# Feed-forward of a Mamba and experts block: input chain half a group sooner, experts' rows gathered one group further ahead

## What is computed

```python
x = L0_attn_x                                   # 4 x 1024 x 256
x = layernorm(x + attn(x, ...))                 # Mamba-2 mixer, then 8 experts, top 2 of them per token
gate = silu((x @ w_gate) * s_gate)              # w_gate, w_up: 256 x 1024 int8
up = (x @ w_up) * s_up
x = layernorm(x + ((gate * up) @ w_down) * s_down)   # w_down: 1024 x 256 int8
```

## Time and profile before

| what | us |
|---|---|
| median of 3 runs (lowest, highest) | 1287.54 (1282.08, 1289.09) |
| profiled execution: its time | 1287.96 |
| profiled execution: its span | 1286.4 |
| TensorE matmul busy in the span | 1135.1 (88%) |
| VectorE, ScalarE, POOL busy | 687.0, 620.7, 369.0 |
| mean granted clock of TensorE | 0.953 |

### The profile page before, as it was taken

How to read it: one execution, slowest core, us unless ns; L and a number is a source line. 1 busy time by engine, 2 the same in 40 slices (tenths; PEclk the granted TensorE clock), 3 DMA queues, 4 the chain that set the end, 5 groups by cost and what they waited for, 6 DMA issues and landing times. The chain is left out here.

```text
span 1286.4 us, 21831 instructions
## 1 busy us (share of the span) xinstructions
PE 1135.1 (88%) x7496; PEld 1001.3 (78%) x7497; DVE 687.0 (53%) x1645; ACT 620.7 (48%) x1279; POOL 369.0 (29%) x328
## 2 busy tenths in 40 slices
PE   0799999899989998899999999999999268888896
PEld 0576768686767686799999999999999247777785
DVE  3576667676767665765322332332332256777654
ACT  1664656555555543354554454454454144444453
POOL 1203133333434243464321304044000432333300
PEclk9899999999999989889999999999999678889898
DMA  2020101010202011263313133121211321121101
GB/s 104 5 70 1 38 1 66 5 67 5 70 1 70 12 43 66 82 219 134 106 41 114 41 108 112 41 106 57 98 41 48 121 72 49 49 83 49 50 18 49
DMA packets 40386, 80.88 MB, mean 63 GB/s; under 512 B 6656, under 2 KB 30080, under 8 KB 39040
## 3 DMA queue, kind: packets, MB, share of 16 engines
q1 hardware_dynamic: 22816, 34.69, 8.2%
q0 software_dynamic: 7440, 35.66, 8.1%
q10 hardware_dynamic: 10064, 9.70, 2.2%
HBM read 48.31 MB, written 30.67 MB: 61 GB/s over the span
## 5 line engine op out<-in xcount | busy, mean ns | idle before, releaser
L1320 DVE TENSOR_TENSOR e_h_lo<-e_bank,e_h_hi 128x512 fp32r<-128x512 f32 x148 | 102.1, 691 | 287.8 <-ACT e_bank L641 285.3
L973 PE MATMUL e_bank<-e_x_hi,e_w_hi 128*128 128x256 f32 x592 | 169.7, 287 | 1.5 <-issue 1.3
L990 PE MATMUL e_bank<-e_w_hi,e_h_hi 128*128 128x256 f32 x592 | 170.6, 288 | 0.0
L974 PE MATMUL e_bank<-e_x_lo,e_w_hi 128*128 128x256 f32 x592 | 168.5, 285 | 0.0
L975 PE MATMUL e_bank<-e_x_hi,e_w_lo 128*128 128x256 f32 x592 | 168.4, 285 | 0.0
L992 PE MATMUL e_bank<-e_w_hi,e_h_lo 128*128 128x256 f32 x592 | 167.6, 283 | 0.0
L991 PE MATMUL e_bank<-e_w_lo,e_h_hi 128*128 128x256 f32 x592 | 167.5, 283 | 0.0
L1639 PE MATMUL f_bank<-f_x_hi,ffn_w 128*128 128x512 f32 x256 | 113.0, 441 | 31.4 <-DVE f_x_lo L1735 28.7
L639 ACT ACTIVATE e_h_hi<-e_bank 128x512 fp32r<-128x512 f32 x148 | 88.5, 598 | 78.4 <-PE e_bank L975 74.6
L1184 DVE SCALAR_TENSOR_TENSOR conv<-raw,conv_w,conv 128x512 f32<-128x512 f32 x120 | 96.0, 801 | 41.6 <-ACT conv L559 38.6
L973 PEld LDWEIGHTS e_bank<-e_x_hi,e_w_hi 128*128 128x128 f32 x592 | 114.5, 193 | 3.1 <-issue 3.1
(11 more groups left out here) (238 smaller groups left out, 2752.6 us busy)
## 6 DMA issues: line engine op xcount, KB each, us to landing
e_stage<-in_w POOLq DMA_DIRECT2D x9, 2048.0 KB
e_x_rows<-sent_rows SPq DMA_DIRECT2D x38, 256.0 KB
back_rows<-e_y_rows ACTq DMA_DIRECT2D x37, 256.0 KB, 2.1
x_in<-in_x SPq DMA_DIRECT2D x8, 512.0 KB, 4.0
x_res_dram<-x_res SPq DMA_DIRECT2D x8, 512.0 KB, 2.9
f_res<-x_res_dram SPq DMA_DIRECT2D x8, 512.0 KB, 3.4
out<-f_out_t SPq DMA_DIRECT2D x8, 512.0 KB, 2.8
back_rows<-zeros SPq DMA_DIRECT2D x8, 256.0 KB, 3.2
```

Source lines behind the costliest of these rows:

```text
L973: mm(out, w1h[:, k, t], x_hi[:, k], start=k == 0, stop=False)
L974: mm(out, w1h[:, k, t], x_lo[:, k], start=False, stop=False)
L990: mm(out, eh_hi[:, k, t], w2h[:, k], start=k == 0, stop=False)
L1320: tt(flat(eh_lo[:, 2 * p:2 * p + 2]), h_ps[p][:], flat(eh_hi[:, 2 * p:2 * p + 2]).bitcast(F32), ALU.subtract).then_inc(es["h_lo_ready"], 1)
```

## The change

The tile `mixed` gets a second buffer, and `mix_first(g)` waits for the normalizing of group g-2 instead of g-1. ScalarE normalizes the next group behind unit 1 instead of 3 and makes its high parts behind unit 4 instead of 6; TensorE transposes behind unit 2 instead of 4. In VectorE's `between` the mix for group g+2 moves to slots 1 and 2, its stats to slot 3, its moments to slot 7 and the shift to slot 0 of the next group; `x_parts` to slot 4. In group 0 the mix and the stats stand four slots later. POOL does `deviation(1)` and `gather(2)` ahead of its loop, and in the loop `gather(g + 3)` stands ahead of the `deviation` of group g+2.

```diff
--- before.py
+++ after.py
@@ -1481,7 +1481,7 @@
         s_down = sb("s_down", [P, D])
         back = sb("back", [P, 2, CH, 2, D])
         res = sb("res", [P, 2, CH, D])
-        mixed = sb("mixed", [P, CH, D])
+        mixed = sb("mixed", [P, 2, CH, D])
         bn = sb("bn", [P, 2, CH, 6])
         mv = sb("mv", [P, CH, 2])
         norm = sb("norm", [P, 3, CH])
@@ -1550,13 +1550,15 @@
             gather(0)
             gather(1)
             deviation(0, norm, "var_ready", "x1_ready", "rs_ready")
+            deviation(1, norm, "var_ready", "x1_ready", "rs_ready")
+            gather(2)
             for g in range(NG + 2):
-                if g + 1 < NG:
-                    deviation(g + 1, norm, "var_ready", "x1_ready", "rs_ready")
                 if g >= 2:
                     deviation(g - 2, norm2, "var2_ready", "out_ready", "rs2_ready")
+                if g + 3 < NG:
+                    gather(g + 3)
                 if g + 2 < NG:
-                    gather(g + 2)
+                    deviation(g + 2, norm, "var_ready", "x1_ready", "rs_ready")
 
         @block.scalar
         def _(act):
@@ -1573,7 +1575,7 @@
                 act.wait_ge(s["shift_ready"], g + 1)
                 if g >= X1_BUFS:
                     act.wait_ge(s["y_ready"], g - X1_BUFS + 1)
-                normalize(x1[:, g % X1_BUFS], mixed, norm, "x1_ready")
+                normalize(x1[:, g % X1_BUFS], mixed[:, g % 2], norm, "x1_ready")
 
             def scale2(g):
                 act.wait_ge(s["shift2_ready"], g + 1)
@@ -1602,9 +1604,9 @@
                     .then_inc(s["gate_ready"], 1)
                 if n:
                     part(n - 1)
-                if f == 3 and g + 1 < NG:
+                if f == 1 and g + 1 < NG:
                     scale1(g + 1)
-                if f == 6 and g + 1 < NG:
+                if f == 4 and g + 1 < NG:
                     x_parts(g + 1)
                 if f == 3 and g >= 2:
                     scale2(g - 2)
@@ -1661,7 +1663,7 @@
                     if g and 1 <= f <= KF // 2:
                         down(g - 1, 2 * f - 2)
                         down(g - 1, 2 * f - 1)
-                    if f == 4 and g + 1 < NG:
+                    if f == 2 and g + 1 < NG:
                         transposes(g + 1)
             for f in range(KF):
                 down(NG - 1, f)
@@ -1674,18 +1676,18 @@
             def mix_first(g):
                 dve.wait_ge(s[f"back_in{g % 2}"], 16 * 2 * CH * (g // 2 + 1))
                 dve.wait_ge(s[f"res_in{g % 2}"], 16 * (g // 2 + 1))
-                if g:
-                    dve.wait_ge(s["x1_ready"], g)
+                if g >= 2:
+                    dve.wait_ge(s["x1_ready"], g - 1)
                 for c in range(CH):
-                    i = stt(mixed[:, c], back[:, g % 2, c, 0], share[:, 0, CH * g + c:CH * g + c + 1],
+                    i = stt(mixed[:, g % 2, c], back[:, g % 2, c, 0], share[:, 0, CH * g + c:CH * g + c + 1],
                             res[:, g % 2, c], ALU.mult, ALU.add)
                 i.then_inc(s["mixed_one"], 1)
 
             def mix_second(g):
                 dve.wait_ge(s["mixed_one"], g + 1)
                 for c in range(CH):
-                    i = stt(mixed[:, c], back[:, g % 2, c, 1], share[:, 1, CH * g + c:CH * g + c + 1],
-                            mixed[:, c], ALU.mult, ALU.add)
+                    i = stt(mixed[:, g % 2, c], back[:, g % 2, c, 1], share[:, 1, CH * g + c:CH * g + c + 1],
+                            mixed[:, g % 2, c], ALU.mult, ALU.add)
                 i.then_inc(s["mixed_both"], 1)
 
             def stats(g, n, x, ready, done):
@@ -1753,41 +1755,42 @@
             def between(g, f):
 
                 if f == 0:
-                    if g >= 2:
-                        y_moments(g - 2)
-                    if g + 1 < NG:
-                        mix_moments(g + 1)
-                if f == 2:
                     if g + 1 < NG:
                         mix_shift(g + 1)
                     if g >= 2:
-                        y_shift(g - 2)
+                        y_moments(g - 2)
+                late = 4 if g == 0 else 0
+                if f == 1 + late and g + 2 < NG:
+                    mix_first(g + 2)
+                if f == 2 and g >= 2:
+                    y_shift(g - 2)
+                if f == 2 + late and g + 2 < NG:
+                    mix_second(g + 2)
                 if f == 3 and 1 <= g <= NG:
                     scale_down(g - 1, 0)
-                if f == 4 and g + 2 < NG:
-                    mix_first(g + 2)
-                if f == 5:
-                    if 1 <= g <= NG:
-                        scale_down(g - 1, 1)
-                    if g + 2 < NG:
-                        mix_second(g + 2)
+                if f == 3 + late and g + 2 < NG:
+                    stats(g + 2, 0, mixed[:, g % 2], "mixed_both", "mix_stats")
+                if f == 4 and g + 1 < NG:
+                    x_parts(g + 1)
+                if f == 5 and 1 <= g <= NG:
+                    scale_down(g - 1, 1)
                 if f == 6 and 1 <= g <= NG:
                     add_x1(g - 1)
-                if f == 7 and 1 <= g <= NG:
-                    stats(g - 1, 1, y[:, (g - 1) % 2], "y_ready", "y_stats")
-                if f == 6 and g + 1 < NG:
-                    x_parts(g + 1)
-                if f == 7 and g + 2 < NG:
-                    stats(g + 2, 0, mixed, "mixed_both", "mix_stats")
+                if f == 7:
+                    if g + 2 < NG:
+                        mix_moments(g + 2)
+                    if 1 <= g <= NG:
+                        stats(g - 1, 1, y[:, (g - 1) % 2], "y_ready", "y_stats")
 
             mix_first(0)
             mix_second(0)
-            stats(0, 0, mixed, "mixed_both", "mix_stats")
+            stats(0, 0, mixed[:, 0], "mixed_both", "mix_stats")
             mix_moments(0)
             mix_shift(0)
             mix_first(1)
             mix_second(1)
-            stats(1, 0, mixed, "mixed_both", "mix_stats")
+            stats(1, 0, mixed[:, 1], "mixed_both", "mix_stats")
+            mix_moments(1)
             x_parts(0)
             for n in range(NG * KF):
                 fuse(n)
```

## The result

| | before | after |
|---|---|---|
| median of 4 runs (lowest, highest) | 1284.88 (1282.08, 1289.09) | 1239.09 (1236.63, 1245.51) |
| profiled execution: time, span | 1287.96, 1286.4 | 1236.63, 1235.0 |
| first gather to the end of the span | 277.34 | 233.11 |

After takes 0.9649 of the time of before (95%: 0.9599 to 0.9698), 45.8 us less by the medians; a second measurement of the same two kernels, in the second series of experiments, gave 0.9668 (0.9634 to 0.9703), 1240.09 against 1284.21. The forecast was 1246, 41.7 us less than the 1287.54 of the first three runs. Of the 51.4 us between the two spans, 7.2 lie ahead of the feed-forward: in code that is the same, the first gather began at 1009.06 and at 1001.89 us. The change owns the **44.2 us** behind it, and all that follows is measured from there, as "the stage".

What follows compares the result with a forecast made beforehand. TensorE was taken as the bound, with x_lo waits at group starts and slow clock behind them. Gains of 1.1, 7.0, 2.8, 29.1 and 1.7 sum to 41.7 us, giving 1246; own range 1240 to 1252, widened to 1239 to 1256.

Steps and rivals of the forecast that it cites:

- head: Before the first unit: second mix needs only its rows, so x_lo is ready at 1036.4 instead of 1037.6, 1.1 us sooner.
- group 0: First group: from 24.98 us to 18.0, summed from units, transposes, their wait and a slow first unit; gain 7.0 us.
- group 1: Second group: from 29.91 us to 27.1, being 23.4 plus 2.0 of waits and 1.7 of slow clock; gain 2.8 us.
- groups 2 to 6: Middle groups: 23.4 us each without x_lo waits or slow clock, from 146.07 us to 117.0; gain 29.1 us.
- group 7 to the end: Last group: starts without idle and loses its slow stretch, priced like the tail's; gain 1.7 us, tail untouched.
- The walk through the queues: VectorE's queue in a middle group, slot by slot: x_lo ready at 18.4 us, needed at 23.4, 5 us to spare.
- its tightest place: Down product's first block: residue of unit 7 done at 28.3 us, wanted at 28.8, 0.5 us of slack.
- 8 times 0.2 for the slow first unit: Group 0's first unit: slow clock on its eight matmuls, a term in the group's 18.0 us.
- The wait that moves to the down block: First rival, down product's first block in every group: 1.2 us idle and 1.7 slow clock, 14.5 us, 1261; chance 0.1.
- The third, the port: Rival: each of a group's eight mixing instructions held 0.95 us for a gather, VectorE becomes the bound, 1272; chance 0.03.
- The second rival's place: POOL's pow held by gathers, VectorE's shift in slot 0 late before every fuse; slower, 1298 us; chance 0.02.
- the fourth, no effect: Rival: x_lo at group starts still late through some overlooked wait, 1286 us; chance 0.03.

Runs made afterwards that it cites:

- 0.6 us of load: Kernel after plus one VectorE multiplication of 512 columns that nobody reads in slot 7 of groups 0 to 7: stage 238.44 us.
- one buffer: Kernel after with one buffer of mixed rows and mix_first waiting for the group before: stage 250.50 us (disturbed), repeated 235.88 us, 0.9698 of before.
- the gathers alone: Kernel before with only POOL's new order, gathering group g+3 in turn g: 0.9939 of before, stage 273.05 us.
- 13 us of load: Kernel after plus twelve POOL pows that nobody reads ahead of the gathers of each of groups 3 to 7: stage 252.38 us.
- the parts back: Kernel after with scale1 behind unit 3, transposes behind unit 4 and both x_parts at unit 6 again: stage 247.87 us, group 0 disturbed.
- the mix put back: Kernel after with VectorE's mix for group g+2 back in slots 4 and 5, its stats in slot 7: stage 261.25 us, with stray waits.

## Why the prediction was right

Its sign, its mechanism and its size hold: x_lo's waits and the slow clock behind them are gone, and the gain is 45.8 us by the medians where 41.7 were forecast. That the absolute time is inside the range of 1239 to 1256 is luck in part: 1239.09 lies 0.1 us from its lower end and outside the forecast's own 1240 to 1252. Of the 6.9 us between it and 1246, 2.7 are the base, since with the fourth run the median of before is 1284.88 instead of 1287.54; 2.5 are terms of the sum, and the rest is what the medians gained beyond the stage. Term by term, in the stage:

| term | predicted gain | measured |
|---|---|---|
| head | 1.1 | 1.2 |
| group 0 | 7.0 | 6.2 |
| group 1 | 2.8 | 4.4 |
| groups 2 to 6 | 29.1 | 29.2 |
| group 7 to the end | 1.7 | 3.2 |
| sum | 41.7 | 44.2 |

**Groups 2 to 6** carry the forecast: 23.4 us a group was worked out from one side by counting matmuls and from the other by taking wait and slow clock from group 1 before, and 23.37 came. The walk through the queues held to 0.4 us at every point shown above, and its tightest place is real: 0.5 us of slack worked out, 0.26 in the rows of after, and 0.6 us of load turned it into a wait.

One reading of the prediction does not hold: that the 6.22 us at 0.50 in group 1 came behind the wait of 3.06 us. The clock had fallen before that wait, at 1059.85, behind the wait of 2.75 us that ended at 1059.24, and stayed low through both, 10.24 us in all. The second matmul from there is already as long as those at the lower level:

```profile
1060.20 0.63 PE L1640 MATMUL f_bank<-f_x_lo,ffn_w 128*128 128x512 f32 x1
```

As a price per wait, 3.1 us was the dearest case; in groups 2 to 6 it was 1.7 to 3.0. The sum did not suffer, since it took the middle groups' time from their starts.

**Group 1** was mis-sized. The step that failed is "TensorE waits in group 1 for a fuse (0.8) and for the last residue (1.2): 2.0 us, and ... 3.4 us of slow clock behind it". The waits are

```profile
1052.91 0.50 PE L1641 MATMUL f_bank<-f_x_hi,ffn_w 128*128 128x512 f32 x1 [0.57 <-DVE f_fused L1746]
1056.73 0.38 PE L1654 MATMUL f_bank<-ffn_w,f_f_hi 128*128 128x256 f32 x1 [0.96 <-DVE f_f_lo L1752]
```

1.5 us, and the clock stayed at 1.00. That it might was in the range, at 1.7 us. (The group is 2.1 us longer than a middle one, more than its waits, which are counted from modelled ends.)

**Group 0** came out 0.8 us short. The step was "8 times 0.2 for the slow first unit", 1.6 us. In the profiled execution the clock stayed at 0.50 beyond the first unit, for 4.9 us from the group's start, which cost 2.4:

```profile
1034.98 0.61 PE L1641 MATMUL f_bank<-f_x_hi,ffn_w 128*128 128x512 f32 x1
1035.40 0.42 PE L1642 MATMUL f_bank<-f_x_lo,ffn_w 128*128 128x512 f32 x1
```

(At the lower level such a row is 0.63 us long, at the upper 0.40.) That is the 0.8 us. When the clock rises differs between executions: with one buffer it did so 3.3 us into the group, and the group took 18.07.

**The tail** gave 1.5 us more than group 7's own slow stretch. Before and after have nearly the same two waits there, 0.57 and 1.41 against 0.55 and 1.39 us; before, 3.4 us at 0.51 followed, after it is 1.00 (the last stretch above). "The tail behind the last unit is untouched" was true of the code and not of the clock. These 1.5 us are luck and no gain of the change: behind such a wait of 1.4 us in the tail the clock fell in 3 of the 10 profiles that have one, in before, in one buffer's two, and in none of the others, the gathers alone among them.

The 1.6 us from these 44.2 to the 45.8 of the medians are inside the spread of the executions: the first gather starts anywhere from 1001.6 to 1019.6 us in the profiles of this study, in code that is the same in all.

**The rivals.** The wait that moves to the down block did not come, but it was the right first rival: 0.6 us more on VectorE calls it up. What the prediction held against it, that no such wait showed before, proved little. Before, the residue was ready 5.1 us into a group too, but TensorE came to it only 7.0 to 8.3 us in, being slowed by the clock; the change takes this time away with the slow clock. The third, the port, did not come either. Beside gathers, four mixes took 1.70 and 1.66 us, against 1.67 without them; of the four gathers issued meanwhile, two took 1.17 and 1.33 instead of 0.95. Over the whole profile, 47 single mixing instructions beside a gather have a median of 475 ns and at most 518, the 17 apart from gathers 477; the gathers' mean rose from 0.96 to 1.02 us. The Trainium skill (SBUF — State Buffer, the section SBUF: two separate sides) has a VectorE instruction with two inputs in SBUF and a GpSimd instruction that reads SBUF exclude each other, the later one blocked for the whole of the other. These rows do not agree for VectorE, and show for single gathers 0.2 to 0.5 us; whether issuing a gather counts as such an instruction, no run here shows. POOL had 8.67 us to spare. The second rival's place was reached only with 13 us of load, and the fourth, no effect, did not come.

**What each part is worth.** Alone, the gathers bring 4.3 us of stage. Taken out of the whole, they cost 41.4, the early mix some 26 to 28, the early parts 1.1 a group and the second buffer 1.8. These don't add up, as they are steps of one chain: rows, then mix, then x_lo. The mix early and nothing else, in the kernel before, was not tried.

## What to carry to other kernels

Walk the in-order queue of the engine that feeds the bottleneck, slot by slot, with the durations and the overlap of the trace: it gave every middle group to 0.1 us and named the place where a further 0.6 us of work costs 0.5 a group. A step can only be moved forward if its data come forward too; here the gathers alone brought 4.3 us of 44, and all the rest without them 2.5. Count the slow clock behind a wait as a second cost that may vanish with it. When it does, the bottleneck comes to its other operands earlier too (here 1.6 to 2.9 us to the last residue), so what never waited before may wait then. Measure from the stage's own start, since the same code ahead of it varies by more than single edits do.

## What was not expected of the hardware

**Where the clock falls.** The granted clock behind each wait of TensorE in the stage, over all profiles: behind single waits of at most 1.31 us it stayed at 1.00 each time (0.77 us in each of six groups of one run and 1.30 in each of five of another among them). Waits close together are another matter: with the parts back, waits of 1.42 and 1.01 us stood 1.2 us apart in the disturbed group 0, and the clock fell 0.35 us behind the second. Behind 1.4 to 2.3 us it went either way: with nearly the same wait of 2.22 to 2.26 us in the run of the mix put back, 3.4 us at the lower level followed in two groups and none in three. From 2.49 us on, the lower level followed or went on every time. Up to 6.2 us of it stood behind the wait of a group's start, and between two waits close together it did not end, as in group 0 of before. Prices from single cases: waits of 1.30 us made their groups 1.6 longer, those of 3.48 and 3.72 us ahead of groups 2 and 4 of before cost 5.2 and 6.7 with the slow clock, and 1.4 us in the tail cost 1.4 or 3.1. Why the middle sizes differ is open.

**Stray waits.** Three of the four profiles of the first series had waits of ScalarE and VectorE whose releaser the trace calls remote, up to 7.6 us each, in two of them in the experts' part too; before, after and the seven runs of the two later series had none. The first profile of one buffer was 15 us longer in the stage than the second, of the same code. They are not spread at random: in one buffer and in the mix put back they stand at ScalarE's gate of unit 4 in several groups in a row, and the second profile of one buffer has none there. What they are is open.
